# A spacer of 480 bytes in front of the multilayer part's rounded weights becomes one of 96 bytes

## What is computed

```
E, H, HID = 512, 16, 2048
x = x + xattn(layernorm(x), ctx)          # ctx 25088 x 512; sigmoid scores; 16 heads of 32
x = x + attn(layernorm(x))                # causal, no softmax, scaled by exp(-n)
lin = lambda x, w, s: einsum('bsi,oi->bso', x, w) * s      # w holds -1, 0 and 1 alone
h = silu(lin(x, w1, s1)) * lin(x, w2, s2)                  # layer 1: 512 -> 2048, twice
h = gelu(lin(h, h1, sh1))                                  # layer 2: 2048 -> 2048
h = gelu(lin(h, h2, sh2))                                  # layer 3: 2048 -> 2048
x = x + lin(h, w3, s3)                                     # layer 4: 2048 -> 512
```

## Time and profile before

| | |
|---|---|
| median of 3 runs | 1901.48 us (1900.17 to 1907.79) |
| time of the profiled execution | 1900.17 us |
| its span, first to last instruction | 1898.5 us |
| TensorE busy | 1885.9 us, 99% |
| VectorE, ScalarE busy | 64%, 53% |
| granted TensorE clock, mean of the core | 1.00 |

### The profile page before, as it was taken

One profiled execution on the slowest core, in us unless ns is written; L12 is line 12 of the kernel. 1 busy time (PEld: TensorE's weight loads), 2 busy tenths in 40 slices (PEclk: granted clock), 3 DMA queues, 4 the chain that ended last, 5 costly groups with the idle time before them and its releaser, 6 DMA issues.

```text
span 1898.5 us, 50956 instructions
## 1 busy us (share of the span) xinstructions
PE 1885.9 (99%) x19424; PEld 1707.8 (90%) x19424; DVE 1213.4 (64%) x2131; ACT 1015.4 (53%) x1141; POOL 5.4 (0%) x19
## 2 busy tenths in 40 slices
PE   9999999999999999999999999999999999999999
PEld 8899999998898999999889899999998989878998
DVE  7676666667667666666766766666676675566322
ACT  6455455554545545555454554555545455555864
POOL 0000000000000000000000000000000000000000
PEclk9999999999999999999999999999999999999999
DMA  7566465565655655566565564555655555545784
GB/s 227 153 150 177 130 157 156 157 162 152 159 147 156 169 133 156 156 158 162 151 161 146 155 172 130 156 156 156 162 152 159 146 157 136 136 138 219 282 298 165
DMA packets 130875, 310.92 MB, mean 164 GB/s; under 512 B 33936, under 2 KB 37008, under 8 KB 112272
## 3 DMA queue, kind: packets, MB, share of 16 engines
q1 hardware_dynamic: 96352, 207.54, 41.3%
q10 hardware_dynamic: 34480, 102.78, 17.3%
HBM read 153.95 MB, written 0.52 MB: 81 GB/s over the span
## 4 chain that ended last, share of the span: by engine, by line
PE 98%; DVE 1%; DMA 1%; ACT 0%; issue 0%; ACTq 0%; SPq 0%; DVEq 0%
PE kp L836 25%; PE vp L861 24%; PE sc L877 20%; PE acc L897 18%; PE ps L1681 6%; PE ps L1666 2%; PE py L1694 1%; PE qk_p L1382 1%; PE vp L945 0%; DMA k_stack_r<-k_stack_r 0%; PE sc L962 0%; DMA probs<-wkT_dram 0%; PE kp L925 0%; PE qk_p L1446 0%; DVE st L1297 0%; DVE ln_stats L72 0%
## 5 line engine op out<-in xcount | busy, mean ns | idle before, releaser
L400 ACT ACTIVATE probs<-sc 128x1024 f32<-128x1024 f32 x784 | 770.4, 1026 | 735.1 <-PE sc L877 578.3
L836 PE MATMUL kp<-x_combos,weights_r 128*128 128x256 f32 x4032 | 521.7, 278 | 0.0
L861 PE MATMUL vp<-more_weights,x_combos 128*128 128x256 f32 x4032 | 513.1, 276 | 0.0
L836 PEld LDWEIGHTS kp<-x_combos,weights_r 128*128 128x128 f32 x4032 | 486.6, 188 | 9.8 <-issue 9.5
L861 PEld LDWEIGHTS vp<-more_weights,x_combos 128*128 128x128 f32 x4032 | 482.9, 188 | 0.6 <-issue 0.4
L877 PE MATMUL sc<-rows_r,k_stack_r 96*128 96x256 f32 x3136 | 436.8, 280 | 2.3 <-ACT probs L400 1.8
L877 PEld LDWEIGHTS sc<-rows_r,k_stack_r 96*128 96x128 f32 x3136 | 393.1, 188 | 24.5 <-issue 20.6
L897 PE MATMUL acc<-probs,v 128*32 128x256 f32 x6272 | 354.4, 380 | 0.0
L625 DVE TENSOR_TENSOR parts<-parts,kp 128x512 f32<-128x512 f32 x240 | 164.5, 686 | 278.3 <-PE kp L836 278.3
L897 PEld LDWEIGHTS acc<-probs,v 128*32 128x32 f32 x6272 | 195.9, 110 | 131.4
L562 DVE TENSOR_TENSOR x_combos<-ctx_raw,x_combos 128x512 fp32r<-128x512 f32 x240 | 166.1, 692 | 8.2
(11 more groups left out here) (209 smaller groups left out, 882.0 us busy)
## 6 DMA issues: line engine op xcount, KB each, us to landing
k_stack_r<-k_rows_hi SPq DMA_DIRECT2D x784, 64.0 KB, 2.3
k_stack_r<-k_rows_lo SPq DMA_DIRECT2D x784, 64.0 KB, 2.5
k_stack_r<-k_stack_r SPq DMA_DIRECT2D x196, 256.0 KB, 3.0
ctx_raw<-ctxT_dram ACTq DMA_DIRECT2D x48, 1024.0 KB, 6.2
weights<-w_all_dram ACTq DMA_DIRECT2D x176, 256.0 KB, 3.7
w_raw<-w_all_dram SPq DMA_DIRECT2D x44, 1024.0 KB, 4.8
weights<-wqk_dram ACTq DMA_DIRECT2D x2, 1024.0 KB, 13.4
probs<-wvT_dram SPq DMA_DIRECT2D x2, 512.0 KB, 7.7
```

The lines of the kernel that those rows point to most:

```text
L400: nc.scalar.activation(probs[:, place(par, n), :], sc[g % 2][:], ACT.Sigmoid).then_inc(probs_ready, 1)
L836: last = nc.tensor.matmul(k2[:, r, :], wk[i - 1][:, k, a, r * P:(r + 1) * P], xc[:, i - 1, k, b, :], start=i in FRESH and r == 0 and n == ...
L861: last = nc.tensor.matmul(v2[:, r, :], xc[:, i - 1, k, b, r * P:(r + 1) * P], wv_c[i - 1][:, k, a, :], start=i in FRESH and r == 0 and n == 0,
```

## The change

The spacer `before_w_hi` has 24 floats instead of 120. `w_hi`, `w_lo` and all that is declared behind them begin 384 bytes lower: `scales`, `s3_sb`, `h_lo1`, `hf`, `gate` and `y` of the multilayer part, and `bo_sb`, `qT`, `n_inv`, `heads`, `n_rows`, `mask`, `st`, `cT`, `cT_part0`, `cT_part1`, `rows_of_zeros` of the self attention. `w_raw`, `weights_r`, `rows_r` and everything of the cross attention stay.

```
@@ -1739,7 +1739,7 @@
         cross_attention(nc, x, ctxT, wqT, wkT, wvT, woT, wqk, wv, bv, wo, w_all, (wn, bqk, bn), keep)
         keep |= {"any_inexact": sb("any_inexact", [1, 1], mybir.dt.int32), "inexact_ready": sem("any_inexact_ready"),
                  "x2": sb("x2", [P, LT, E]), "raw": sb("w_raw", [P, RING, UNIT]),
-                 "before_w_hi": sb("before_w_hi", [P, 120]), "w_hi": sb("w_hi", [P, RING, UNIT], F32R), "w_lo": sb("w_lo", [P, RING, UNIT], F32R),
+                 "before_w_hi": sb("before_w_hi", [P, 24]), "w_hi": sb("w_hi", [P, RING, UNIT], F32R), "w_lo": sb("w_lo", [P, RING, UNIT], F32R),
                  "scales": sb("scales", [P, 4, KH]), "s3": sb("s3_sb", [P, E]), "scales_loaded": sem("scales_ld"),
```

## The result

The changed kernel takes 1905.97 us in the median of 9 runs (1905.24 to 1907.54), the kernel before on the same chip 1900.42 in 9 runs. The ratio is 1.0028, with a 95% interval of 1.0019 to 1.0036: 0.28% slower, clear of no change, and under the 0.5% that I had named as a bound. Forecast was 1906.4 us, 0.26% slower, on a median of 1901.5 us for the kernel before that three runs had given.

A forecast was written before the change was run, and what follows sets the result against it. TensorE's spacing of matmul starts was taken to bound the kernel. Layers 1 and 2 at 3.5 us plus layer 3 at 1.4, all else 0, gave 4.9 on a median of 1901.5: 1906.4 us, range 1899.5 to 1910.0.

The forecast's parts named there:

- The bound: TensorE, busy 99% of the span, sets the end; any change in spacing between matmul starts arrives there whole.
- Layers 1 and 2: 768 matmuls go from distance 192 to 64 and run at 117.9 instead of 113.3 ns: 3.5 us, bounds 0 and 5.1.
- The step from 48 slow matmuls in a row to 768: First-chunk keys and values stay at 117.9 ns for 48 matmuls; layers 1 and 2 were taken to stay so for 768.
- The step on how an idle TensorE starts: Layer 1, starting from rest, was taken as slow like the last chunk, not fast like after weighing V: 3.5 us or 0.
- At distance 192 a stream reaches 113.3 by itself: Read from layer 1 before the change: after an idle TensorE its 256 matmuls lose only 0.12 us.
- the loop of the cross attention: Scores' products at distance 192 follow each pair of distance-64 products, and were taken to return the stream to 113.3 ns.
- Layer 3: 256 matmuls with `rows_r` slow, 1.2 us, plus 0.2 for those with `h_lo1` finding the pace again: 1.4, between 0 and 3.1.
- Layer 4: 64 matmuls of 512 columns go from distance -192 to -64: -0.1 to +0.3 us, taken as 0.
- Self attention, ScalarE and VectorE: Moved self attention operands taken as 0, within 0.3 us; ScalarE and VectorE accesses taken as 0, hidden by TensorE.
- The first: Rival, not slower: layer 1's stream is fast at distance 64 too, or distance plays no part; 1901.5 us, chance 0.29.
- The second: Rival, slower by more: layer 3's alternating distances, or that of layers 1 and 2, run at 120 ns; 1910.1 us, chance 0.07.
- The third: Rival, faster: the next weights' load gets out of the way and spacing falls; by 4 ns gives 1896.4 us, chance 0.04.

The follow-up runs named there:

- e1_only_w: On the changed kernel, a spacer of 96 floats behind `w_lo` leaves only `w_hi` and `w_lo` 384 bytes lower; 1905.89 us, ratio to before 1.0027.
- e9_mid_seed: The changed kernel with 16 extra matmuls at distance 192 behind the first 128 matmuls of layer 1, none ahead of it; one execution, 1906.38 us.
- e3_seed_plain: The changed kernel with 16 extra matmuls at distance 192 ahead of layer 1, weights at 0 and rows at 192; median 1907.7 us, ratio 1.004.
- e11_seed_plain_again: The kernel of e3_seed_plain, the changed kernel with 16 extra matmuls ahead of layer 1, run once more unchanged for its scattered times; 1905.56 us.

## Why the prediction was right

**The bound.** TensorE has no idle time in the part, and the loss in its spacing arrived at the end whole: 5.5 us by the layers, 5.4 in the span, 5.55 in the medians.

**The total is nearer than the sum.** 1906.4 us forecast and 1905.97 measured are 0.4 apart, but partly by luck: the loss was 0.6 us larger than the 4.9 forecast, and the median of the kernel before, with nine runs instead of three, came out 1.1 us lower than the 1901.5 that it was added to.

**Layers 1 and 2: 3.5 us forecast, 3.4 measured** (1.13 + 2.27), at 117.8 ns against 117.9 read off. The step from 48 slow matmuls in a row to 768 held: the spacing repeats without drift until layer 3. The step on how an idle TensorE starts held too, though it was a guess: a choice between two kinds of rows, and the earlier trace rows, and 0 or 3.5 us hung on it. The start from rest at distance 64 is slow in all three kernels that have it, the changed one, e1_only_w and e9_mid_seed.

**"At distance 192 a stream reaches 113.3 by itself" was too strong.** From rest it does, in the two kernels with that distance in layer 1. In layer 3 of the changed kernel every other long stretch with `h_lo1` stays slow for all its 14 matmuls, in the kernels with the extra matmuls a stretch at 192 is slow right behind a fast one at 64, and next to stretches at 448 none at 192 gets fast. Which pace a stream gets depends on what came before it, at both distances. What I wrote of the loop of the cross attention, that scores at 192 return it to 113.3, stays a reading of the rows; no run took the scores away.

**Layer 3: 1.4 us forecast (0 to 3.1), 1.86 measured.** The 256 matmuls with `rows_r` run slow as taken, 256 x 4.5 = 1.15 us. The term that was too small is the one of the 256 with `h_lo1`: 0.2 taken for finding the pace again, 0.7 measured, since half of their long stretches don't find it.

**Layer 4: 0 forecast (-0.1 to 0.3), 0.28 measured** from start to start, 14.42 to 14.70 us: the top of the bound from the earlier trace rows. Self attention, ScalarE and VectorE: 0, as taken; the part begins within 0.1 us of where it began in the two profiles, and e1_only_w, in which their tensors are put back, changes nothing in layers 1 and 2.

**The rivals.** The first, a fast stream at distance 64, is possible, as the runs with extra matmuls show, but was never seen from rest. By the rule of the Trainium skill's page "TensorE: Matmul & The Clock Gate", section on the back-to-back issue gap, which gives the spacing by the number of streamed columns and by no address, all of this would be one spacing; here the trace decides against it, with 113.3 to 120.0 ns for one shape at different distances. The second has its pace, 120.0 ns, but at distances 0 and 256, where layers 1 and 2 cost 5.1 us. The third, a pace under 113.3, was seen nowhere.

## What to carry to other kernels

Where TensorE sets the time, look at the spacing of matmul starts and not only at its busy share: 99% busy covers a pace from 113.3 to 120.0 ns here, and what decides is how far apart the staying and the moving operand begin, and how the stream entered. A tensor's place is a parameter like a tile's size: a spacer of some hundred bytes moved 160 us of work by 3.5%, with no instruction changed. When a buffer is moved for another reason, compare the spacing afterwards, in every product that reads it, and above all in those that start from an idle TensorE.

## What was not expected

- At distance 64 a stream of identical matmuls has two paces that last, 117.8 and 113.3 ns, and it goes from the one to the other over 16 matmuls of another distance (e9_mid_seed, at 1751 us of its span).
- Distances 0 and 256 give the same 120.0 ns from rest, and 64 and 320 the same 117.8, but 448 (117.8) is not like 192 (113.3). I have no mechanism for this; that the load of the next weights and the rows that stream meet in SBUF is a guess which no run here tests.
- The part begins at 1733.7 to 1734.4 us in five of the fourteen profiled executions and at 1735.7 to 1736.1 in nine, of one and the same kernel too (1733.67 in e3_seed_plain, 1735.74 in e11_seed_plain_again). The nine, and they alone, have a lower granted clock in the last chunk of the cross attention: 0.83 from 1655 to 1665 us, where the five have 1.00. That is 1.7 of the 10 us. The stretch is that of a weighing of V, 3.59 us in the changed kernel's profile and 4.88 in that of e11_seed_plain_again for the same 64 matmuls. The pieces of the chain of work, of the changed kernel and of e11_seed_plain_again:

```profile
1659.95 3.59 PE acc L897 x64
```

```profile
1660.20 4.88 PE acc L897 x64
```

And the stretches (TensorE's busy time, the clock, DMA share, GB/s), again first of the changed kernel, then of e11_seed_plain_again:

```profile
1655.00:1665.00 10.00, 8.22 (x100) 1.00 0.90 261
```

```profile
1655.00:1665.00 10.00, 8.22 (x86) 0.83 0.90 262
1661.00:1662.00 1.00, 1.00 (x16) 0.50 0.83 287
```

From 1661 to 1662 us the clock is at 0.50, the lower of its two levels (1.2 GHz instead of 2.4). TensorE is partly idle just before, busy 3.22 of the 5 us from 1655 to 1660, in both executions; why the clock falls in one and not in the other isn't shown. The fall is as large as a third of the change's effect, so single executions of this kernel are compared by their layers, not by their totals.
